# A four-layer network on one core: second layer's routing logits in four groups between the attention lanes' first projections

## The chip, the cores and the metric

The kernel runs on one core of a Trainium2 chip. The time is the device time of one execution, in microseconds. Five engines have a queue of instructions each, carried out in order: TensorE (PE, whose weight loads are shown apart as PEld), VectorE (DVE), ScalarE (ACT), GpSimd (POOL), and SyncE (SP), which issues DMAs. An instruction can wait for a semaphore that another engine raises; whatever stands behind it in its queue waits with it.

## The reference, cut to what matters

Four layers follow one another on 2048 rows of 128 numbers. Each layer normalises the rows (`xn = (x - mean) / sqrt(var + eps)`), computes an attention branch `s` and a feed-forward branch `g` from them, and ends with `x = x + s * g`. The second layer is the one touched:

```
# attention branch, 8 batches of 256 rows
xn2 = layernorm(xn) * ln_scale + ln_bias
hid = silu(xn2 @ W_hidden + b_hidden)          # 128 -> 512
v, gate = hid[..., :256], hid[..., 256:]
qk  = silu(xn2 @ W_qk + b_qk)                  # 128 -> 128
q, k = qk * os_weight[0] + os_bias[0], qk * os_weight[1] + os_bias[1]
a   = square(relu(q @ k.T / 256))
s   = ((a @ v) * gate) @ W_out + b_out
# feed-forward branch: 8 experts, top 2, at most 320 rows an expert
logits = xn @ Wr + br
w = softmax(top 2 of logits); each expert keeps its 320 greatest weights
g = silu(layernorm(xn + sum of the chosen experts' weighted outputs) * gamma + beta)
```

## The kernel before, in words

A stage is a class with one generator for each engine. `Net.run` weaves the generators of its stages: for each engine it takes one step of each generator in turn, up to the next `yield`, until all are through. So a `yield` fixes the order of the instructions in an engine's queue, and nothing else does: there is no planner. A round below is one turn of this weaving; the rounds of PE, DVE and ACT are counted each by themselves, from the start of one `n.run(...)`.

The second layer (`layer1`, L2159) runs, in this order: `Norms` (both normalisations of the rows: `xn` by DVE, the doubly normalised `t1` by ACT), `Turn` as `n.turn` (PE turns `xn` in four quarters of 512 rows through PSUM banks 4 to 7, and DVE copies them into `xT`), `Turn` as `n.inner` (the same for `t1`, banks 0 to 3, copied by ACT into `tT` with gain and bias, L595), and then one run that weaves three stages, `n.run(route, *lanes)`.

**The lanes** are two `SquaredAttention` stages (L1729). Lane 0 takes batches 0, 2, 4, 6 in banks 0 to 2, lane 1 takes 1, 3, 5, 7 in banks 3 to 5 and begins one round later (`later`). On PE a lane has four steps for a batch: the first projections (`qk` L1769, `v` L1771, `gate` L1774), the scores (L1779), their product with `v` (L1786), the output projection (L1793). On DVE it has, after an empty first step, the bias of `v` (L1836), the square (L1839), the gating (L1845), the output rows (L1848); each needs the PE step of its own kind, and the PE step that follows it needs it: the square is needed by the product with `v`, the gating by the output projection, the rows by the next batch's first projections. The scores need `k`, which ACT makes (L1808).

**The routing** is `Route1` (L1926). PE: the 16 logits products of 128 rows each into bank 6 (`pe_logits`, L645), two yields, 16 transposes of the spread weights in two steps (L1961), then eight steps with one count each (L1967), the threshold's product (L1971), and the ranks (L1975, L705, L706). DVE: the logits with bias (L651), the top two, the pair softmax, the spread, copies of the turned weights, and eight rounds of a search for each expert's threshold: in each, DVE reads back the count before (L2040, L2043), sets a candidate (L2032), compares 2048 numbers with it (L2035), and writes `hit` (L2037), which the count on PE needs; after the search the ranks and slots, and the map of rows (`RowMap`), whose last cast (L1922) releases the gathers of the experts' rows on POOL (L1196). DVE takes the routing's step, then lane 0's, then lane 1's in each round, and `hit` of count s (from 0 to 7) is written in its round 5 + s. On PE the order of stages in a round is the same.

In the listing, PE's queue is built by `SquaredAttention.pe_steps` and `Route1.pe`.

Of the kernel before, what the change touches and what calls it, by code (L numbers as in the profile page):

```python
# [13 lines left out]
NB, NS = 8, 256  # L14
NT = NB * NS // P
TOK = NB * NS
E = 8
# [38 lines left out]
def later(lane, idle):  # L56

    for _ in range(idle):
        yield
    yield from lane  # L60
# [176 lines left out]
class Stage:  # L237
# [9 lines left out]
    def pe(self):  # L247
        yield
# [381 lines left out]
class Router(Stage):  # L630
# [9 lines left out]
    def pe_logits(self, tileT, weight, sources, bank):  # L640
        pe, k = self.tensor, weight.shape[1]
        for s in sources:
            pe.wait_ge(*s)
        for t in range(NT):
            ins = pe.matmul(self.n.bank(bank)[:, t * k:(t + 1) * k], tileT(t), weight, start=True, stop=True)  # L645
        ins.then_inc(*self.lg_mm.up())
# [54 lines left out]
    def pe_prefix(self, k, marks, bank):  # L701
        pe, ps = self.tensor, self.n.bank(bank)
        flat = marks[:, :, :].rearrange("p t e -> p (t e)")
        pe.wait_ge(*self.asked.at(k))
        pe.matmul(ps[:, 0:128], self.c["before"], flat, start=True, stop=True)  # L705
        pe.matmul(ps[:, 128:256], self.c["ones"], flat, start=True, stop=True).then_inc(*self.summed.up())  # L706
# [210 lines left out]
class GeluExperts(Stage):  # L917
# [53 lines left out]

    def pe(self):
        pe, N, bank, tb, yb = self.tensor, self.TILES, self.n.bank, self.turn_banks, self.y_banks
        for s in self.sources:
            pe.wait_ge(*s)
# [753 lines left out]
class SquaredAttention(Stage):  # L1729
# [30 lines left out]
    def pe_steps(self):  # L1760
        n, pe, w1 = self.n, self.tensor, self.n.w1
        b0, b1, b2 = self.banks
        for q in range(4):
            pe.wait_ge(*n.inner.done(q))
        for i, b in enumerate(self.batches):
            tT = n.tT[:, b * NS:(b + 1) * NS]
            if i:
                pe.wait_ge(*self.rows.at(i - 1))
            pe.matmul(b2[:, 0:NS], w1["qk"], tT, start=True, stop=True).then_inc(*self.qk_mm.up())  # L1769
            for r in range(2):  # L1770
                ins = pe.matmul(b1[:, r * NS:(r + 1) * NS], tT[:, r * 128:(r + 1) * 128], w1["hidden"][:, 0:256], start=True, stop=True)  # L1771
            ins.then_inc(*self.v_mm.up())
            for f in range(2):
                ins = pe.matmul(b0[:, f * NS:(f + 1) * NS], w1["hidden"][:, 256 + 128 * f:384 + 128 * f], tT, start=True, stop=True)  # L1774
            ins.then_inc(*self.gate_mm.up())
            yield
            pe.wait_ge(*self.k.at(i))
            for r in range(2):
                ins = pe.matmul(b2[:, r * NS:(r + 1) * NS], self.kk[:, r * 128:(r + 1) * 128], self.qT, start=True, stop=True)  # L1779
            ins.then_inc(*self.scores.up())  # L1780
            yield
            pe.wait_ge(*self.a.at(i))
            pe.wait_ge(*self.v_silu.at(i))
            for f in range(2):
                for j in range(2):
                    ins = pe.matmul(b0[:, f * NS:(f + 1) * NS], self.vb[:, j * NS + f * 128:j * NS + f * 128 + 128],  # L1786
                                    self.ab[:, j * NS:(j + 1) * NS], start=(j == 0), stop=(j == 1))
            ins.then_inc(*self.av.up())
            yield
            pe.wait_ge(*self.gated.at(i))  # L1790
            for r in range(2):
                for f in range(2):
                    ins = pe.matmul(b2[:, r * 128:(r + 1) * 128], self.ogT[:, f * NS + r * 128:f * NS + r * 128 + 128],  # L1793
                                    w1["out"][:, f * 128:(f + 1) * 128], start=(f == 0), stop=(f == 1))
            ins.then_inc(*self.out_mm.up())
            yield
# [129 lines left out]
class Route1(Router):  # L1926
# [23 lines left out]

    def pe(self):
        n, pe, c = self.n, self.tensor, self.c
        self.pe_logits(n.xT_tile, n.w1["router"], [n.turn.done(q) for q in range(4)] + [n.w_in["w1"].at(0)], 6)
        yield
        yield
        for q in range(4):
            pe.wait_ge(*(self.spread_a if q >= 2 else self.spread_d).at(0))
            if q >= 2:
                pe.wait_ge(*(self.out_a if q % 2 else self.out_d).at(0))
            for r in range(4):  # L1960
                ins = pe.transpose(n.bank(6 + q % 2)[:, r * 128:(r + 1) * 128], n.t1[:, 4 * q + r, :], c["ident"])  # L1961
            ins.then_inc(*self.turned.up())
            if q % 2:
                yield
        for s in range(8):
            pe.wait_ge(*self.reached.at(s + 1))
            pe.matmul(n.bank(7, 1), c["digit_sum"], self.hit, start=True, stop=True).then_inc(*self.counted.up())  # L1967
            yield
        pe.wait_ge(*self.reached.at(9))
        for i in range(2):  # L1970
            ins = pe.matmul(n.bank(7)[:, 8 * i:8 * i + 8], self.both16[:, 128 * i:128 * i + 128], c["digit_first"], start=True, stop=True)  # L1971
        ins.then_inc(*self.counted.up())
        yield
        pe.wait_ge(*self.reached.at(10))
        pe.matmul(n.bank(7, E), c["ones"], n.e8[0][:, :], start=True, stop=True).then_inc(*self.counted.up())  # L1975
        self.pe_prefix(0, n.tie, 6)
        yield
        self.pe_prefix(1, n.k8[4], 6)
        yield from later(self.map.pe(), 3)
# [179 lines left out]
def layer1(n, before):  # L2159
    norms = Norms(n, n.xn, n.t1, lambda t: [before.done(t)])  # L2160
    n.run(norms)
    n.turn = Turn(n, n.xn, lambda q: n.xT[:, 2 * q:2 * q + 2, 1:1 + NS], norms.once_done, banks=(4, 5, 6, 7), by_dve=(0, 1, 2, 3))
    n.run(n.turn)
    n.inner = Turn(n, n.t1, lambda q: n.tT[:, q * 512:(q + 1) * 512], norms.twice_done, n.w1["ln_g"], n.w1["ln_b"])
    n.run(n.inner)
    kept = KeepRows(n, [norms.once_done(NT - 1)])
    n.run(kept)
    route = Route1(n)
    lanes = [SquaredAttention(n, lane, range(lane, NB, 2), lane) for lane in range(2)]
    n.run(route, *lanes)  # L2170
    experts = FullExperts(n, n.ys[1], [lane.done() for lane in lanes], [n.cleared[1].at(0), kept.kept.at(0), route.map.made.at(0)], route.map)
    n.run(experts)
    got = Back(n, [n.t1, n.g], n.ys[1], experts.done(), "full")
    n.run(got)
    norm = WeightedNorm(n, n.t1, n.g, lambda t: [got.done(t)])
    n.run(norm)
    n.run(Ready(n, ACT.Silu))
    gate = TurnedGate(n, norm.done, n.w1["gamma"], n.w1["beta"])
    n.run(gate)
    return gate  # L2180
# [1575 lines left out]
def build(nc, ins, out):  # L3756
    n = Net(nc, ins, out.rearrange("(t p) c -> p t c", p=P))
    before = layer0(n)
    before = layer1(n, before)
    n.run(Load3(n))  # L3760
    before = layer2(n, before)
    layer3(n, before)
# [103 lines left out]
```

## Time and profile before

| | us |
|---|---|
| three runs | 917.67, 923.87, 923.76 |
| median | 923.76 |
| span of the profiled execution | 921.0 |
| PE busy | 692.4 (75%) |
| DVE busy | 595.3 (65%) |
| ACT busy | 399.3 (43%) |
| POOL busy | 292.5 (32%) |
| second layer's weaving of routing and lanes | 235.6 to 315 |

The three runs bear no mark that tells which of them the profile belongs to; the span is counted from the first to the last instruction, and the median lies 2.8 us above it. The shares are averages over four layers that are each limited by something else, so they say little about one stage. In the traces, a matmul on 32-bit numbers stands as two records, so that the 16 logits products are shown as "x32".

### The profile page before, as it was taken

How to read it: one execution, taken by the hardware profiler on the slowest of the kernel's cores; microseconds unless marked ns; L12 is line 12 of the kernel's file. 1: busy time of each engine (PE TensorE's matmuls, PEld its weight loads, DVE VectorE, ACT ScalarE, POOL GpSimd, SP SyncE). 2: the span in 40 equal slices, each digit the busy share in tenths (PEclk: the TensorE clock that was granted, in tenths of full speed). 3: DMA queues.
4: the chain of work that ended last, by engine and by line, in shares of the span. 5: the costliest groups of instructions: out<-in, count | busy, mean ns of one | idle time of the engine just before them, and what ended most of it. 6: DMA issues, size and time to landing. Idle time of an engine off the chain costs nothing. (4 is left out here: it accounts for less than half of the span.)

```text
span 921.0 us, 14463 instructions
## 1 busy us (share of the span) xinstructions
PE 692.4 (75%) x4255; PEld 516.3 (56%) x4255; DVE 595.3 (65%) x1590; ACT 399.3 (43%) x990; POOL 292.5 (32%) x303
## 2 busy tenths in 40 slices
PE   4999866743979379328986988999976677749991
PEld 2999834632767248327875674656544444426560
DVE  4797487538688611286667567889947665636685
ACT  3201334534735123164444446767756333326660
POOL 1373143540000265300100002445410555665552
PEclk9999878865799779768997899999997699969996
DMA  9991001220100140319008431222100122112515
GB/s 286 244 281 77 1 27 44 68 69 0 47 0 1 11 47 9 93 51 391 1 1 156 124 86 34 75 78 73 53 25 17 48 61 60 57 54 57 163 58 141
DMA packets 79564, 72.97 MB, mean 79 GB/s; under 512 B 9618, under 2 KB 73885, under 8 KB 78977
## 3 DMA queue, kind: packets, MB, share of 16 engines
q1 hardware_dynamic: 68000, 57.56, 23.3%
q0 software_dynamic: 7072, 12.40, 5.2%
q10 hardware_dynamic: 4416, 2.10, 0.9%
q8 instruction: 37, 0.61, 0.3%
q14 instruction: 39, 0.31, 0.1%
HBM read 42.85 MB, written 27.46 MB: 76 GB/s over the span
## 5 line engine op out<-in xcount | busy, mean ns | idle before, releaser
L3493 POOL DMA_INDIRECT ys<-work,back_to x78 | 78.9, 1011 | 83.7 <-DVE work L3452 38.0
L3336 PE MATMUL banks<-weights,work 128*128 x156 | 91.6, 673 | 7.8 <-issue 6.2
L2535 DVE TENSOR_REDUCE work<-banks 128x2 f32<-128x512 f32 x128 | 83.5, 683 | 14.4 <-PE banks L2526 13.1
L3349 PEld LDWEIGHTS banks<-consts,work 128*128 128x128 f32 x156 | 21.8, 155 | 79.4 <-issue 52.5
L3359 PE MATMUL banks<-weights,work 128*128 x312 | 54.8, 303 | 5.4 <-DVE work L3452 3.2
L3349 PE MATMUL banks<-consts,work 128*128 128x128 f32 x156 | 34.3, 305 | 32.1 <-DVE work L3441 15.5
L816 POOL DMA_INDIRECT xs<-t,idx x48 | 49.1, 1023 | 28.7 <-DMA ys<-work,back_to 15.4
L2526 PE MATMUL banks<-work 96*128 96x256 bf16 x256 | 49.3, 277 | 9.1 <-DVE work L2535 6.0
L1196 POOL DMA_INDIRECT g<-rows,back_to x16 | 15.3, 958 | 120.4 <-DVE back_to L1922 115.8
L3359 PEld LDWEIGHTS banks<-weights,work 128*128 128x128 f32 x312 | 46.2, 213 | 8.1 <-issue 7.7
L2939 PE MATMUL banks<-work 99*128 99x256 bf16 x256 | 48.7, 275 | 1.7 <-issue 1.6
L3391 ACT ACTIVATE work<-work 128x256 f32<-128x256 f32 x39 | 16.2, 415 | 69.2 <-DVE work L3429 51.4
L3427 DVE TENSOR_TENSOR work<-banks,weights 128x512 f32<-128x512 f32 x39 | 27.0, 692 | 24.1 <-PE banks L3336 10.9
L816 POOL DMA_INDIRECT xs<-weights,idx x32 | 31.4, 982 | 28.2 <-PE banks L2939 25.7
L3033 ACT ACTIVATE tT<-banks 128x512 f32<-128x512 f32 x64 | 36.5, 598 | 7.5 <-PE banks L2939 5.2
L885 PE MATMUL banks<-consts,g 128*128 128x128 f32 x32 | 7.4, 427 | 41.3 <-DVE g L417 41.3
L2526 PEld LDWEIGHTS banks<-work 96*128 96x128 bf16 x256 | 20.8, 98 | 28.3 <-DVE work L2535 12.6
L3336 PEld LDWEIGHTS banks<-weights,work 128*128 128x128 f32 x156 | 25.8, 207 | 15.6 <-issue 14.8
L567 PE MATMUL banks<-consts,xn 128*128 128x128 f32 x48 | 11.7, 438 | 29.7 <-DVE xn L417 20.1
L3377 ACT ACTIVATE work<-banks,weights 128x128 f32<-128x128 f32 x74 | 30.6, 414 | 7.7 <-PE banks L3317 5.2
L3033 ACT ACTIVATE weights<-banks 128x512 f32<-128x512 f32 x48 | 28.5, 593 | 11.8 <-PE banks L2939 10.5
L1161 ACT ACTIVATE work<-banks,weights 128x320 f32<-128x320 f32 x32 | 16.3, 527 | 39.7 <-PE banks L1135 19.2
(508 smaller groups left out, 1946.1 us busy)
## 6 DMA issues: line engine op xcount, KB each, us to landing
weights<-in_w SPq DMA_DIRECT2D x1, 6668.0 KB, 19.6
weights<-in_w SPq DMA_DIRECT2D x1, 4569.5 KB, 33.8
work<-xs SPq DMA_DIRECT2D x62, 64.5 KB
weights<-in_r SPq DMA_DIRECT2D x1, 2950.5 KB, 26.5
xs<-zero SPq DMA_DIRECT2D x1, 2600.0 KB, 26.1
xs<-zero SPq DMA_DIRECT2D x1, 2580.0 KB, 33.5
work<-xs SPq DMA_DIRECT2D x39, 65.0 KB
weights<-in_w SPq DMA_DIRECT2D x1, 2124.5 KB, 12.1
```

Source lines behind the costliest of these rows:

```text
L816: g.indirect_dma_start(self.table[:, :], bass.IndirectOffsetOnAxis(ap=idx[:, j, t:t + 1], axis=0), self.rows[:, t, :], None, **more).then_ ...
L1161: a.activation(self.hid[e % 2][:, f, :], n.bank(2 + f, cap), ACT.Gelu, bias=n.w1["b1"][:, 4 * e + f:4 * e + f + 1]).then_inc(*self.a.up())
L2526: ins = pe.matmul(ps[:, r * NS:(r + 1) * NS], q[0:self.ROWS, h * NS + r * 128:h * NS + r * 128 + 128], k[0:self.ROWS, h * NS:(h + 1) * NS] ...
L2535: v.tensor_reduce(self.mxb[:, 2 * h:2 * h + 2], self.n.bank(bank).rearrange("p (r n) -> p r n", r=2), AX, ALU.max, negate=True).then_inc(* ...
L2939: ins = pe.matmul(ps[:, kt * NS:(kt + 1) * NS], k[0:h.ROWS + 3, hd * NS + kt * 128:hd * NS + kt * 128 + 128], q[0:h.ROWS + 3, hd * NS:(hd ...
L3033: a.activation(h.PT[s % 8], bank(2 + s % 3), ACT.Exp, scale=float(np.float32(8.0) ** np.float32(-0.5))).then_inc(*h.exp.up())
L3336: pe.matmul(self.mid(t), self.hT[t % 4], w1[:, bass.ds(off * 4, 512)], start=True, stop=True).then_inc(*self.prod1.up())
L3349: ins = pe.transpose(self.mid(m)[:, 128 * f:128 * f + 128], self.ha[m % 4][:, 128 * f:128 * f + 128], self.c["ident"])
L3359: ins = pe.matmul(self.y_bank(m), self.at_[m % 4][:, 128 * f:128 * f + 128], w2[:, bass.ds(self.pe_off[m] * 2 + 128 * f, 128)], start=(f = ...
L3377: a.activation(self.hT[t % 4], self.turn_bank(t), ACT.Identity, scale=gain, bias=bias).then_inc(*self.xT.up())
L3427: v.tensor_tensor(hm, self.mid(t), n.r3["mlp1_b"][:, bass.ds(off * 4, 512)], ALU.add).then_inc(*self.sum.up())
L3493: g.indirect_dma_start(ys[:, :], bass.IndirectOffsetOnAxis(ap=n.back_to[:, t:t + 1], axis=0), self.yb[t % self.RETURNS], None, bounds_chec ...
```

## The change

`Route1.pe` no longer calls `pe_logits`. It waits for the weights, and then for each quarter q in turn for `n.turn.done(q)` alone, issues the four logits products of that quarter, and yields. The last product raises the same semaphore as before. Of the two yields that followed, one stays. `SquaredAttention.pe_steps` no longer waits for all four quarters of `tT` ahead of everything: each batch waits for the quarter that it lies in, `n.inner.done(b // 2)`. For the first batch of a lane, waits are added for what had used its three banks before (the list `free`), and two yields are added: one between the `v` and the `gate` products, and one between the two `gate` products. In `layer1`, the quarters are turned through the banks in another order. The steps of DVE, ACT, POOL and SP are as before, and so is each product.

```diff
--- before.py
+++ after.py
@@ -1760,18 +1760,24 @@
     def pe_steps(self):
         n, pe, w1 = self.n, self.tensor, self.n.w1
         b0, b1, b2 = self.banks
-        for q in range(4):
-            pe.wait_ge(*n.inner.done(q))
+        free = [n.inner.done(q) for q in range(3)] if self.lane == 0 else [n.turn.done(2), n.turn.done(1), n.inner.done(3)]
         for i, b in enumerate(self.batches):
             tT = n.tT[:, b * NS:(b + 1) * NS]
-            if i:
-                pe.wait_ge(*self.rows.at(i - 1))
+            pe.wait_ge(*n.inner.done(b // 2))
+            pe.wait_ge(*(self.rows.at(i - 1) if i else free[0]))
             pe.matmul(b2[:, 0:NS], w1["qk"], tT, start=True, stop=True).then_inc(*self.qk_mm.up())
+            if i == 0:
+                pe.wait_ge(*free[1])
             for r in range(2):
                 ins = pe.matmul(b1[:, r * NS:(r + 1) * NS], tT[:, r * 128:(r + 1) * 128], w1["hidden"][:, 0:256], start=True, stop=True)
             ins.then_inc(*self.v_mm.up())
+            if i == 0:
+                yield
+                pe.wait_ge(*free[2])
             for f in range(2):
                 ins = pe.matmul(b0[:, f * NS:(f + 1) * NS], w1["hidden"][:, 256 + 128 * f:384 + 128 * f], tT, start=True, stop=True)
+                if i == 0 and f == 0:
+                    yield
             ins.then_inc(*self.gate_mm.up())
             yield
             pe.wait_ge(*self.k.at(i))
@@ -1950,8 +1956,14 @@
 
     def pe(self):
         n, pe, c = self.n, self.tensor, self.c
-        self.pe_logits(n.xT_tile, n.w1["router"], [n.turn.done(q) for q in range(4)] + [n.w_in["w1"].at(0)], 6)
-        yield
+        pe.wait_ge(*n.w_in["w1"].at(0))
+        for q in range(4):
+            pe.wait_ge(*n.turn.done(q))
+            for t in range(4 * q, 4 * q + 4):
+                ins = pe.matmul(n.bank(6)[:, t * E:(t + 1) * E], n.xT_tile(t), n.w1["router"], start=True, stop=True)
+            if q == 3:
+                ins.then_inc(*self.lg_mm.up())
+            yield
         yield
         for q in range(4):
             pe.wait_ge(*(self.spread_a if q >= 2 else self.spread_d).at(0))
@@ -2159,9 +2171,9 @@
 def layer1(n, before):
     norms = Norms(n, n.xn, n.t1, lambda t: [before.done(t)])
     n.run(norms)
-    n.turn = Turn(n, n.xn, lambda q: n.xT[:, 2 * q:2 * q + 2, 1:1 + NS], norms.once_done, banks=(4, 5, 6, 7), by_dve=(0, 1, 2, 3))
+    n.turn = Turn(n, n.xn, lambda q: n.xT[:, 2 * q:2 * q + 2, 1:1 + NS], norms.once_done, banks=(6, 4, 5, 7), by_dve=(0, 1, 2, 3))
     n.run(n.turn)
-    n.inner = Turn(n, n.t1, lambda q: n.tT[:, q * 512:(q + 1) * 512], norms.twice_done, n.w1["ln_g"], n.w1["ln_b"])
+    n.inner = Turn(n, n.t1, lambda q: n.tT[:, q * 512:(q + 1) * 512], norms.twice_done, n.w1["ln_g"], n.w1["ln_b"], banks=(2, 1, 0, 3))
     n.run(n.inner)
     kept = KeepRows(n, [norms.once_done(NT - 1)])
     n.run(kept)
```

## Rows read from the trace of the kernel before

**Rows 1.** Head of the profile's page: the span.
```profile
span 921.0 us, 14463 instructions
```

**Rows 2.** Waits, 228 to 320 us: waiter, waited for, us in total, times, longest.
```profile
POOL g L1196 <- DVE back_to L1922: 115.8, 1, 115.8
...
DVE byexpert L651 <- PE banks L645: 5.2, 1, 5.2
```

**Rows 3.** Timeline 228 to 246 us: start, duration, engine, line, operation, idle before.
```profile
234.57 2.76 ACT L595 ACTIVATE tT<-banks,weights 128x512 f32<-128x512 f32 x4
235.61 4.42 PE L645 MATMUL banks<-weights,xT 128*128 128x8 f32 x32
...
239.88 1.20 PE L1769 MATMUL banks<-tT,weights 128*128 128x256 f32 x2
240.14 0.29 DVE L651 TENSOR_TENSOR byexpert<-banks,weights 128x128 f32<-128x128 f32 x1 [5.15 <-PE banks L645]
...
240.88 1.91 PE L1771 MATMUL banks<-weights,tT 128*128 128x256 f32 x4
...
245.55 0.59 PE L1769 MATMUL banks<-tT,weights 128*128 128x256 f32 x2
```

**Rows 4.** Timeline, 258.9 to 288 us: first and last of eight counts, one round between.
```profile
258.90 0.15 DVE L2037 TENSOR_SCALAR work<-work 128x1 f32<-128x1 f32 x1
...
275.16 0.15 DVE L2037 TENSOR_SCALAR work<-work 128x1 f32<-128x1 f32 x1
275.23 0.41 DVE L1848 TENSOR_TENSOR s<-banks,weights 128x256 f32<-128x256 f32 x1
...
275.37 0.38 PE L1967 MATMUL banks<-work,consts 128*128 128x1 f32 x2 [0.74 <-DVE work L2037]
275.56 0.68 DVE L1845 TENSOR_TENSOR work<-banks,work 128x512 f32<-128x512 f32 x1
...
275.70 0.70 PE L1769 MATMUL banks<-tT,weights 128*128 128x256 f32 x2
...
276.16 0.15 DVE L2040 TENSOR_SCALAR work<-banks 128x1 int32<-128x1 f32 x1
...
276.73 2.35 DVE L2035 TENSOR_SCALAR_CACHE_REDUCE work<-work 128x2048 bf16<-128x2048 f32 x1
...
277.96 1.05 PE L1793 MATMUL banks<-weights,work 128*128 128x128 f32 x8
...
279.12 0.15 DVE L2037 TENSOR_SCALAR work<-work 128x1 f32<-128x1 f32 x1
...
287.33 0.15 DVE L2037 TENSOR_SCALAR work<-work 128x1 f32<-128x1 f32 x1
```

**Rows 5.** Timeline, 267 to 271 us: the other two steps of a lane on PE.
```profile
267.46 1.99 PE L1786 MATMUL banks<-work 128*128 128x256 f32 x8 [0.22 <-DVE work L1839]
...
269.29 1.03 PE L1779 MATMUL banks<-work 128*128 128x256 f32 x4
```

**Rows 6.** Timeline, 314 to 316 us: the map's last cast, the first gather.
```profile
314.63 0.18 DVE L1922 TENSOR_SCALAR back_to<-back_to 128x20 int32<-128x20 int32 x1
...
315.64 0.99 POOL L1196 DMA_INDIRECT g<-rows,back_to  x1 [115.83 <-DVE back_to L1922]
```

**Rows 7.** Windows: stretch, length, busy us of each engine, granted clock, DMA.
```profile
236.00:237.00 1.00, 1.00 (x12) 1.00 (x11) 0.00 (x0) 1.00 (x3) 0.00 (x0) 1.00 1.02 291
...
144.00:148.00 4.00, 1.45 (x9) 0.97 (x8) 1.01 (x2) 1.81 (x3) 1.93 (x2) 1.00 0.15 50
258.90:289.40 30.50, 25.67 (x130) 21.03 (x131) 29.46 (x63) 13.62 (x28) 0.00 (x0) 1.00 0.00 1
761.33:764.43 3.10, 0.00 (x1) 0.01 (x1) 1.99 (x6) 0.49 (x2) 1.93 (x4) 0.92 0.05 17
764.43:767.30 2.87, 2.87 (x9) 2.12 (x10) 1.92 (x6) 1.58 (x7) 2.26 (x3) 0.50 0.21 60
...
784.29:787.60 3.31, 3.31 (x9) 2.15 (x10) 1.92 (x6) 1.64 (x7) 2.70 (x3) 0.51 0.23 69
```

## The prediction

> **What bounds the kernel now.** I read four views. First the page's head, for the span of 921.0 us [rows 1]. Then the waits of the stretch that the change touches: POOL stands still for 115.8 us until DVE's cast L1922 [rows 2], and the first gather starts 1 us after it [rows 6]. Nothing else of the second layer follows before that gather, so whatever moves L1922 moves everything behind it. The last rows of a lane (L1848) stand directly behind L1922 in DVE's queue and aren't the later bound by more than their own 0.4 us. Then the timeline from the logits on: PE turns out the 16 logits products between 235.61 and 240.03, DVE waits 5.15 us for them, and only then does PE take lane 0's first projection, at 239.88 [rows 3]. This is the wait that stands out, and quarters of `tT` had been arriving since 235.2 (ACT's four copies begin at 234.57 and take 2.76 us [rows 3]).
>
> Last the timeline of the eight counts [rows 4]: `hit` is written at 258.90 and for the eighth time at 287.33, so a round takes 28.43 / 7 = 4.06 us. In the round shown, DVE writes `hit` (275.16), does lane 0's rows and lane 1's gating, and reads the count back at 276.16, without having waited: PE did the count at 275.37, in 0.38 us, **while** DVE worked for the lanes, and took the lanes' own steps (L1769 at 275.70 and so on) while DVE compared (2.35 us). DVE is busy 29.46 of 30.5 us there, PE 25.67, and the clock is granted in full, 1.00, which is 2.4 GHz [rows 7]. So this stretch is bound by DVE, and only because PE's part of each round lies under the compare.
>
> **The order that the change writes.** PE's queue comes from counting yields. Before, lane 0's step k is in round k, lane 1's in round k+1 (the steps being projections, scores, product, output, projections, ...), and count s in round 5+s. After, a lane's first step takes three rounds, so all later steps come 2 rounds later. The routing's logits take four rounds and one bare yield follows, where there were two rounds: its transposes, counts and the rest come 3 rounds later. DVE's order is not touched. So on PE, the routing slips **one round behind the lanes**:
>
> - before, ahead of count s stand lane 0's step 4+s and lane 1's step 3+s. What these need of DVE stands ahead of compare s.
> - after, ahead of count s stand lane 0's step 5+s and lane 1's step 4+s. These need DVE's step 4+s for lane 0 and 3+s for lane 1, which stand **behind** `hit` s in DVE's queue.
>
> There is no deadlock in it, but a chain: `hit` s, DVE's lane step, PE's step of lane 0, PE's step of lane 1, count s, read back, next compare. What ran beside the compare now runs between two compares, and DVE waits for it with everything queued behind its read-back: the next candidate, compare, and both lanes' steps, hence ACT and PE too.
>
> **A round, priced.** From the end of PE's count to the next `hit` is 0.05 us, then from L2040 to L2035 0.57 us (276.16 to 276.73), the compare with its readout 2.39 us (276.73 to 279.12) [rows 4], in all 3.0. A PE step at full clock takes, from its start to the start of the next: projections 2.26 us (275.70 to 277.96) [rows 4], product 1.83 us (267.46 to 269.29), scores 0.83 and output 0.85 us (their 1.03 and 1.05 less the 0.2 by which successive records overlap) [rows 4, 5]. DVE's lane steps are 0.41 or 0.68 us [rows 4]. Four kinds of round take turns:
>
> - rows, then projections and output: 0.5 + 2.26 + 0.85 + 0.38 + 3.0 = 7.0
> - `v` bias and rows, then lane 1's projections (scores lie under the compare): 1.15 + 2.26 + 0.38 + 3.0 = 6.8
> - square, then product and scores: 0.8 + 1.83 + 0.83 + 0.38 + 3.0 = 6.85
> - gating, then output and product: 0.8 + 0.85 + 1.83 + 0.38 + 3.0 = 6.85
>
> The mean is 6.9 us against 4.06: +2.85 for each of 7 rounds, **+20.0**. Four more waits of the same form follow while lanes still have steps: for the eighth count, the threshold's product, the free places with the first prefix, and the second prefix. Each has a pair of lane steps ahead of it, less what DVE did beside it: 2.65 each, **+10.6**. The row map comes after the lanes' last products and doesn't change.
>
> **The start.** Ahead of the last logits group, PE's queue now holds lane 0's whole first step, and `qk`, `v` and half of `gate` of lane 1. DVE's first routing step needs all four groups, and lane 0's DVE steps stand behind it. At full clock a projection step has 0.59 + two pairs at about 1.03; [rows 3] show 0.59 at 245.55. A logits group is 8 records, at the 12 records a microsecond of 236 to 237 us [rows 7] 0.7 us. Sum: 4 x 0.7 + 2 x 0.59 + 2.06 + 1.03 + 0.5 = 7.6, so the logits end at 243.2 instead of 240.03: +3.2. At half clock, which the before trace has there from 240 on (L1769 as 1.20 and L1771 as 1.91 us [rows 3]), the same list takes 11.3 us: +6.9. I take **+3.2**, since wide products now come between the narrow ones from the start, while the clock stands at 1.00 [rows 7]; +6.9 is kept for the range. The transposes of the spread weights get lane 0's product and lane 1's scores ahead of them: **+0.5**, most of it under the copies.
>
> **What costs nothing.** The waits on quarters and banks: each is for a copy that ended by 237.33 (234.57 + 2.76 [rows 3]), when PE is 1.7 us into its list. If the third quarter weren't there, lane 0's gate would stand for at most 0.7 us. The new bank order changes no count of transposes; the earlier readers of banks 0 to 2 have been done since before the logits. No DMA and nothing of POOL or SP is moved, so nothing is late on their queues but by L1922. The gain of the change, the first `qk` 3.6 us earlier (236.3 instead of 239.88), lands on ACT, whose next lane work waits for DVE anyway: 0.
>
> Sum without the clock: 20.0 + 10.6 + 3.2 + 0.5 = **+34.3**.
>
> **The clock.** In each round PE now sits idle from the count (or the scores behind it) to DVE's next lane step: 3.0 us plus 0.4 to 0.8 of DVE, 3.4 to 3.8, or some 2.8 where scores follow; twelve such gaps. The trace of before has three gaps of 3.1 to 3.4 us in the last layer, and PE resumed at 0.50 (1.2 GHz) after each: after the one at 761.33 it worked 2.87 us at 0.50 [rows 7], at 784.29 it did so again [rows 7], and a third time at 804. That is 2.87 / 2 = 1.4 us lost. Against it: with only 1.45 us of work in 144 to 148 us, the clock stayed at 1.00 [rows 7]. Bounds: none of twelve, 0; all of twelve, 12 x 1.4 = +16.8. I take half of the gaps, **+8.4**, the gaps being like those that cost, but followed by longer bursts.
>
> The Trainium skill has a rule on this, on the page "TensorE: Matmul & The Clock Gate", in the section on HAM oscillation: a TensorE that waits between bursts falls back to half rate in each wait and starts every burst cold. By it the sum would be the upper bound, and the rows at 764 and 784 us agree with it, those at 144 us don't.
>
> **Forecast**: 921.0 + 34.3 + 8.4 = 963.7 us of span; the median of the runs shown is 2.8 us above the span, so 966.5, **966 us**.
>
> **The rivals.**
>
> - *The clock holds* through the gaps: 921.0 + 34.3 + 2.8 = 958. For it the row at 144; against it the three resumptions at 764, 784 and 804.
> - *The clock falls in every gap*: 963.7 + 8.4 + 2.8 = 975, with the half-clock start 979.
> - *The slipped round is hidden.* DVE would find the counts done as before, and only the later logits remained: 923.8 + 3.2 to 6.9 = 927 to 931. For it: PE has 4.8 us of slack in 30.5. Against it: slack is of use only where PE may run ahead, and the steps ahead of each count need what DVE writes after `hit`.
> - *The lanes gain and carry the end*, the other side. Place: the first projections, price: 239.88 - 236.3 = 3.6 us, 920. It decides if the lanes' last rows, not L1922, release the experts by more than 4 us, and no count stands behind a lane step. Against it: L1922 and the last rows lie together, and POOL waits for L1922.
> - *The change doesn't do what it says*: lane 1 finds its bank or quarter busy. All are free by 237.3; worth under 1 us.
>
> **How the numbers follow.** Forecast 0.42, clock holds 0.27, clock falls always 0.20, slip hidden 0.06, lanes carry the end 0.05. The three first all lie far above 1%, which is about what a measurement of this kernel tells from no change, 933 us being the bound: slower 0.89. Both last lie within 1%, less a little for a real gain: same 0.09, faster 0.02. The range leaves the two last out and takes the others with their bounds: from the clock that holds, less the 6 us that the three runs of before spread over, 952, to 979.
>
> **What would show it.** Right: L1967 starts some 3.5 us after L2037 instead of 0.2; DVE shows waits of 2.5 to 3 us at L2040 for PE L1967, eight times, and its busy share of the counts falls from 97% to under 60%; `hit` comes every 6.8 us or more; L651 starts near 243.5; L1922 ends near 349 to 366. The granted clock of the counts' stretch is between 0.75 and 1.00. Wrong: `hit` every 4.1 us, or L651 at 240, or L1967 still directly behind L2037. Then the order of PE's queue isn't the one I counted.

## The result and the profile after

The change makes the kernel slower. Six runs took 970.15 to 976.42 us, 974.43 us in the median, against 923.62 us for the kernel before beside them; the ratio is 1.0582, with a 95% interval of 1.0547 to 1.0617. All ratios here come from fast runs alone, so they can differ a little from the quotient of the two medians (here 1.055). The span of the profiled execution is 973.8 us. The forecast was 966 us, with a range from 952 to 979.

The head of the page of the kernel after:

```profile
span 973.8 us, 14466 instructions
## 1 busy us (share of the span) xinstructions
PE 713.2 (73%) x4255; PEld 531.4 (55%) x4255; DVE 594.7 (61%) x1590; ACT 400.6 (41%) x990; POOL 293.7 (30%) x303
```

DVE, ACT and POOL do the same work in the same busy time. Only PE is busy for longer, 713.2 instead of 692.4 us, with as many instructions. The added time is waiting, and PE's own work stretched.

The waits of the second layer, 228 to 380 us (waiter, waited for, us in total, times, longest), answer to [rows 2]:

```profile
POOL g L1196 <- DVE back_to L1928: 170.0, 1, 170.0
DVE work L2052 <- PE banks L1979: 35.5, 8, 5.1
...
DVE byexpert L651 <- PE banks L1963: 7.9, 1, 7.9
```

L1928 is the cast that was L1922, L2052 the read-back of a count that was L2040, L1979 the count, L1963 the logits. The second row is new: DVE waits for **all eight counts**, 4.4 us each. Before, it waited for none.

The start, in order of time, answers to [rows 3]:

```profile
232.09 0.96 PE L1963 MATMUL banks<-weights,xT 128*128 128x8 f32 x8
...
232.90 0.68 PE L1768 MATMUL banks<-tT,weights 128*128 128x256 f32 x2
...
238.65 0.95 PE L1963 MATMUL banks<-weights,xT 128*128 128x8 f32 x8
...
239.72 0.29 DVE L651 TENSOR_TENSOR byexpert<-banks,weights 128x128 f32<-128x128 f32 x1 [7.87 <-PE banks L1963]
```

The first projection of lane 0 now follows the first logits by 0.8 us, and the last logits end at 239.60, 7.5 us after the first began. Before, it was 4.4 us.

One round of the search (rounds here from one `hit` to the next) answers to [rows 4]:

```profile
277.60 0.15 DVE L2049 TENSOR_SCALAR work<-work 128x1 f32<-128x1 f32 x1
277.67 0.68 DVE L1845 TENSOR_TENSOR work<-work 128x512 f32<-128x512 f32 x1
278.27 0.69 DVE L1842 TENSOR_TENSOR work<-banks,weights 128x512 f32<-128x512 f32 x1
...
278.41 3.78 PE L1792 MATMUL banks<-work 128*128 128x256 f32 x8 [3.81 <-DVE work L1845]
...
281.98 1.09 PE L1785 MATMUL banks<-work 128*128 128x256 f32 x4
...
282.92 0.28 PE L1979 MATMUL banks<-work,consts 128*128 128x1 f32 x2
...
283.23 0.16 DVE L2052 TENSOR_SCALAR work<-banks 128x1 int32<-128x1 f32 x1 [4.27 <-PE banks L1979]
...
283.81 2.35 DVE L2047 TENSOR_SCALAR_CACHE_REDUCE work<-work 128x2048 bf16<-128x2048 f32 x1
...
286.20 0.15 DVE L2049 TENSOR_SCALAR work<-work 128x1 f32<-128x1 f32 x1
```

`hit` is written at 277.60, but the count that needs it starts at 282.92: PE first takes lane 0's product, which waits for the square that DVE does behind `hit`, and lane 1's scores. Before, the count came 0.2 us after `hit`. While DVE compares (2.35 us), PE has nothing to do. The product takes 3.78 us instead of 1.99 [rows 5]: the granted clock of that burst is 0.51 (below).

The granted clock (column ahead of the last two) over the eight counts, then in one gap of PE and in the burst behind it, then in another such pair:

```profile
261.05:320.76 59.71, 34.56 (x118) 28.34 (x118) 28.13 (x55) 14.30 (x28) 0.00 (x0) 0.73 0.00 0
257.90:261.68 3.78, 0.01 (x2) 0.03 (x1) 3.28 (x6) 0.60 (x1) 0.00 (x0) 0.99 0.00 0
261.68:264.50 2.82, 2.82 (x7) 2.28 (x8) 0.45 (x1) 1.50 (x3) 0.00 (x0) 0.50 0.00 0
...
283.20:287.06 3.86, 0.00 (x1) 0.01 (x1) 3.69 (x8) 1.09 (x2) 0.00 (x0) 0.80 0.00 0
287.06:290.50 3.44, 3.44 (x12) 3.17 (x13) 0.54 (x1) 0.00 (x0) 0.00 (x0) 0.50 0.00 0
```

Before, it was 1.00 for the whole of the counts [rows 7], and the same seven rounds took 28.43 us; now they take 59.71, and DVE's busy share there is 28.13 / 59.71 = 47%, from 97%. The end of the stage answers to [rows 6]:

```profile
365.81 0.18 DVE L1928 TENSOR_SCALAR back_to<-back_to 128x20 int32<-128x20 int32 x1
...
366.81 1.00 POOL L1196 DMA_INDIRECT g<-rows,back_to  x1 [169.97 <-DVE back_to L1928]
```

The bill from these rows, in us:

| | before | after | more |
|---|---|---|---|
| start of the trace to the first logits | 235.61 | 232.09 | -3.5 |
| first logits to first `hit` | 23.29 | 28.96 | +5.7 |
| first to eighth `hit` | 28.43 | 59.71 | +31.3 |
| eighth `hit` to the map's last cast | 27.30 | 45.05 | +17.8 |
| from that cast to the end of the span | 606.4 | 608.0 | +1.6 |
| sum | 921.0 | 973.8 | +52.8 |

The bill compares one profiled execution of each kernel. The first row isn't the change's doing: 3.1 of the 3.5 us lie ahead of the second layer's normalised rows, in code that both share, and the rest lies in the turns, which take from 6.8 to 7.3 us from the first normalised row to the first logits in the traces of kernels that turn first, with either bank order.

### The profile page after: what moved, and what is told of

Its sections match the earlier page's. It is cut to its first block and busy times, and to the rows that moved or that the text cites. A ratio compares the mean times of both kernels' runs of the same rounds, so it can differ in the third digit from the quotient of the medians.

```text
span 973.8 us, 14466 instructions
## 1 busy us (share of the span) xinstructions
PE 713.2 (73%) x4255; PEld 531.4 (55%) x4255; DVE 594.7 (61%) x1590; ACT 400.6 (41%) x990; POOL 293.7 (30%) x303
## 5 line engine op out<-in xcount | busy, mean ns | idle before, releaser
L1792 PE MATMUL banks<-work 128*128 128x256 f32 x64 | 27.2, 601 | 17.4 <-DVE work L1845 17.4
L3415 ACT ACTIVATE work<-banks 128x256 f32<-128x256 f32 x78 | 29.2, 375 | 11.1 <-PE banks L3361 7.8
```

## The experiments

All kernels of a group ran on one chip beside the kernel before. In the first group (four kernels) the kernel before took 881.26 us, in the two later ones 921.37 and 921.13 us; the chips differ by some 4.5%, so ratios are compared, and stretches of the traces, which agree between the chips to some 0.1 us for a round.

**The slip undone.** The change without the one bare yield:

```diff
@@ Route1.pe of the change
             if q == 3:
                 ins.then_inc(*self.lg_mm.up())
             yield
-        yield
         for q in range(4):
```

> The change as it is, with the one bare yield behind the routing's logits on PE taken out, so that counts stand as they did before, relative to the lanes' steps. The groups of logits, the waits on quarters and the lanes' two new yields stay. Theory (the slipped round makes the chain): hit every 4.1 us again instead of 8.5, the granted clock at 1.00 through the counts, and only the later logits remain: 924 to 928 us. Rival (the cost lies in the interleaving itself: groups, new waits, the lanes' longer first step): still above 960 us.

It took 887.6 us, 1.0055 (1.0009 to 1.0100) of before. DVE's `hit`, first and last, and the counts' stretch:

```profile
250.16 0.15 DVE L2048 TENSOR_SCALAR work<-work 128x1 f32<-128x1 f32 x1
...
278.59 0.15 DVE L2048 TENSOR_SCALAR work<-work 128x1 f32<-128x1 f32 x1
```

```profile
250.16:278.59 28.43, 24.11 (x118) 19.53 (x118) 27.49 (x55) 12.99 (x27) 0.00 (x0) 1.00 0.00 1
```

The seven rounds take 28.43 us, to the hundredth what they took before, and the clock is back at 1.00. The groups, the new waits, the bank order and the lanes' two yields stay in this kernel, so none of them makes the 50 us. From the first logits to the first `hit` it takes 26.37 us, 3.1 more than before: this is the whole price of the later logits.

**The slip alone.** The kernel before with one yield more:

```diff
@@ Route1.pe of the kernel before
         self.pe_logits(n.xT_tile, n.w1["router"], ... , 6)
         yield
         yield
+        yield
         for q in range(4):
```

> The kernel before with nothing but one bare yield more behind its logits on PE. Theory: the counts slip one round behind the lanes, hit every 8 us or more, DVE waits for each count, and the clock falls in the gaps: 923.6 + 31 for the chain + 12 to 20 for the clock = 966 to 975 us. Rival (the interleaving costs, not the slip): 924 us.

It took 938.6 us, 1.0674 (1.0611 to 1.0737): 57 us slower, by a line that issues nothing. The waits of DVE from the first to the eighth `hit`, and the stretch:

```profile
DVE work L2041 <- PE banks L1968: 31.7, 7, 5.1
```

```profile
252.65:313.46 60.81, 36.02 (x118) 29.50 (x118) 28.13 (x55) 14.30 (x28) 0.00 (x0) 0.71 0.00 0
```

The loss is in full there with the logits in one block, with `hit` every 60.81 / 7 = 8.69 us. It came out above the 966 to 975 us that were expected of the other chip (42 to 51 us more than before). In its trace the way from the first logits to the map's last cast is 54.9 us longer than before: 4.7 up to the first `hit`, 32.4 in the seven rounds, 17.8 behind them. Less the 31 us given to the chain, 24 are left, where I had given the clock 12 to 20. The next run shows that the clock costs more than that in the change; how the 24 us divide in this kernel was not separated.

**The gaps filled.** The change with idle work on PE, behind each count and the threshold's product:

```diff
@@ Route1 of the change
+    def fill(self, k):
+        n, pe = self.n, self.tensor
+        for _ in range(k):
+            pe.matmul(n.bank(6)[:, 0:256], n.w1["qk"], n.tT[:, 0:256], start=True, stop=True)
...
             pe.matmul(n.bank(7, 1), c["digit_sum"], self.hit, start=True, stop=True).then_inc(*self.counted.up())
+            self.fill(5)
             yield
...
         ins.then_inc(*self.counted.up())
+        self.fill(5)
         yield
```

> The change as it is, with five products of 128x256 without use, into a free bank, behind each of the eight counts and behind the threshold's product (some 2 us of work on PE at full clock, in gaps of 3.1 to 3.9 us). Theory (chain plus clock): the clock stays at 1.00 through the counts, hit every 7.0 us instead of 8.5, so 8 or 9 gaps save 1.5 us each: 974.4 - 13 = 961 us, between 958 and 965. Rival A (half clock in the bursts costs nothing, the chain alone is 8.5 us long): 974 us or more. Rival B (the fill delays the next lane step): above 976 us.

It took 920.31 us, 1.0475 (1.0408 to 1.0542), where the change has, on other chips, 1.0582 and, measured again, 1.0618. The 958 to 965 us expected for the first chip are 1.037 to 1.045 of before, so the ratio lies just above them and the quotient of the medians, 1.044, within. One round of it (L1960 is the fill, L2056 writes `hit`, L1984 is the count), and the counts' stretch:

```profile
263.73 0.15 DVE L2056 TENSOR_SCALAR work<-work 128x1 f32<-128x1 f32 x1
...
264.54 1.99 PE L1792 MATMUL banks<-work 128*128 128x256 f32 x8 [1.55 <-DVE work L1845]
266.37 1.03 PE L1785 MATMUL banks<-work 128*128 128x256 f32 x4
267.23 0.28 PE L1984 MATMUL banks<-work,consts 128*128 128x1 f32 x2
267.37 2.40 PE L1960 MATMUL banks<-tT,weights 128*128 128x256 f32 x10
...
267.55 0.16 DVE L2059 TENSOR_SCALAR work<-banks 128x1 int32<-128x1 f32 x1 [2.46 <-PE banks L1984]
```

```profile
248.42:297.99 49.57, 40.06 (x188) 33.40 (x188) 28.14 (x55) 14.19 (x28) 0.00 (x0) 0.97 0.00 0
```

The product is back at 1.99 us, DVE still waits 2.46 us for the count: this is the chain without the clock's part. The rounds took 8.54 us (the first, its gap lying ahead of the first fill), then 6.77, 6.79, 6.87, 7.04, 6.77 and 6.79 us, against 6.8, 6.85, 6.85 and 7.0 worked out for the four kinds, in the order in which they come here. With the clock falling they take 8.53. So more useless work on PE made the kernel some 10 us faster in this stretch (59.71 - 49.57), and half clock costs 1.7 us a round. From the first logits to the map's last cast it takes 120.57 us, in the change 133.72: 13.1 us less, where 13 were expected. That refutes rival A. Rival B is refuted too: in each of the rounds PE waited again for DVE behind the fill (1.55 us in the one shown). Only the step behind the eighth count stood directly behind its fill, and came 2.4 us after that count instead of 1.7.

**DVE slips too.** The change with one yield more on DVE's side, so that both queues have the routing one round behind:

```diff
@@ Route1.dve of the change
         v.tensor_copy(self.spread(0), ...).then_inc(*self.spread_d.up())
         yield
+        yield
         for q in (0, 2):
```

> The change as it is, with one bare yield more in the routing's steps on DVE, behind the spread, so that DVE's search slips one round behind the lanes as PE's counts do. Theory (what costs is the difference between the orders of the two queues): the chain is broken again, hit every 4.1 to 4.3 us, 924 to 929 us. Rival (the counts stand too late in PE's queue as such, whatever DVE's order is): above 960 us.

It took 885.57 us, 1.0061 (1.0023 to 1.0098), 4.3 us more than before by the medians. From the first logits to the first `hit` it takes 28.0 us, 4.7 more than before, and 0.7 less from there to the map's last cast. A `hit` and the count behind it:

```profile
261.55 0.15 DVE L2050 TENSOR_SCALAR work<-work 128x1 f32<-128x1 f32 x1
261.65 0.69 DVE L1851 TENSOR_TENSOR work<-banks,work 128x512 f32<-128x512 f32 x1
261.75 0.38 PE L1979 MATMUL banks<-work,consts 128*128 128x1 f32 x2 [0.78 <-DVE work L2050]
```

```profile
253.53:282.27 28.74, 23.71 (x116) 18.99 (x116) 27.80 (x55) 11.22 (x23) 0.00 (x0) 1.00 0.00 1
```

PE's queue is here, instruction for instruction, that of the slow kernel. What cost 50 us is not where the counts stand in PE's queue but where they stand relative to the same lanes' steps in DVE's.

**Logits earlier.** No slip; a group of logits stands ahead of each quarter of the inner turn, and the lanes' first steps are whole again:

```diff
@@ layer1 and Route1.pe of the change
-    n.run(n.inner)
+    route = Route1(n)
+    n.run(EarlyLogits(n, route), n.inner)    # its pe(): for q: wait turn.done(q), 4 logits products, yield
...
-        pe.wait_ge(*n.w_in["w1"].at(0))
-        for q in range(4):
-            ...
+        yield
         yield
```

> No slip, and the logits earlier instead of later: a group of logits goes ahead of each quarter of the inner turn, the lanes' first steps are whole again and wait for their own quarters. Theory: the one thing worth having at the start is an earlier end of the logits, since DVE waits 5.2 us for them; PE does the same list, so they end some 1 to 3 us sooner after the first turn, the lanes' first projection hardly moves, hit comes every 4.1 us, and the kernel is 0 to 3 us faster than before: ratio 0.997 to 1.000. Rival (the inner turn, now later, holds up the lanes or the spread, which waits for all four quarters): 1 to 4 us slower than before.

It took 925.12 us against 921.37, 1.0040 (1.0007 to 1.0072). The expectation missed: `hit` comes every 4.06 us, but the logits end no sooner. The time is what the rival gave, 1 to 4 us more; the trace shows the clock as well as the later inner turn. Two windows of the logits and turns in this kernel:

```profile
231.00:236.00 5.00, 5.00 (x26) 5.00 (x26) 1.50 (x3) 1.94 (x5) 0.00 (x0) 0.50 0.73 210
236.00:240.00 4.00, 4.00 (x22) 4.00 (x22) 0.00 (x0) 1.55 (x2) 0.00 (x0) 0.50 0.00 0
```

PE was busy all the time and stayed at 0.50, so that a group took 1.71 us, where it takes 0.95 in the change. From the first normalised row (L485) to L651 it took 14.25 us, before 11.74.

**The change again**, beside it on that chip:

> The change as it is, for its ratio on the same chip as the experiments. Theory: hit every 8.5 us again, falls of the clock in every gap, 1.055 to 1.065 of the time before. Rival (the two chips differ in more than a constant): outside of that.

975.96 us, 1.0618 (1.0567 to 1.0669), `hit` every 8.54 us, DVE waiting 35.5 us in eight waits as in the first trace.

**Fill ahead of the layer.** The kernel before, with sixteen useless products of 128x256 on PE once the first layer's gate is through, and four behind the variance:

```diff
@@ layer1 of the kernel before
     n.run(norms)
+    n.run(Fill(n, norms.variance.at(0)))    # PE: 16 products, wait, 4 products, all into bank 0
```

> The kernel before, with twenty products of 128x256 without use on PE in the 9.6 us in which it is idle ahead of the second layer's turns (sixteen at once, four behind the variance). Theory: before, PE starts that layer at half clock (0.50 until 234.8 us) and is at 0.50 again for the end of the logits; kept busy, it turns and makes the logits at 1.00, so that the logits end some 2 to 3 us sooner after the first turn, with hit every 4.1 us as before: ratio 0.997 (0.994 to 1.000). Rival (the clock falls in the logits whatever stands ahead of them, or DVE and ACT pace the turns anyway): no difference that can be told, ratio 0.998 to 1.003.

922.88 us against 921.13, 1.0002 (0.9969 to 1.0035). The clock was at 1.00 through both turns, as wanted, but then:

```profile
234.00:236.00 2.00, 1.81 (x16) 1.66 (x15) 0.11 (x1) 2.00 (x4) 0.00 (x0) 1.00 1.01 290
236.00:238.00 2.00, 2.00 (x14) 2.00 (x13) 0.00 (x0) 1.75 (x2) 0.00 (x0) 0.63 0.20 57
238.00:240.00 2.00, 2.00 (x9) 1.91 (x9) 0.49 (x2) 0.00 (x0) 0.00 (x0) 0.50 0.00 0
```

it fell within the block of logits, which stand from 234.37 us on without a gap. The logits took 5.0 us instead of 4.4, and L651 came 11.95 us after the first normalised row. The rival holds: no difference can be told. Neither of these two kernels is better than the kernel before, and no better one was found.

## Why the prediction was right, point by point

**The order of the queue** was right, and it is the cause: undone, the loss is gone; alone, it is whole; and given to DVE as well, it is harmless. The sign and the place follow from it.

**A round without the clock** was priced at 6.9 us and took 6.77 to 7.04 with the gaps filled. The +20.0 us for seven rounds stands, as (6.84 - 4.06) x 7 = 19.5.

**The tail's four waits** were priced at +10.6. Measured is +17.8 with the clock's part and +14.7 (42.01 - 27.30) in the filled kernel, whose last two gaps had no fill and were still followed by half clock. Its trace tells the two apart:

```profile
313.66 0.29 DVE L714 COPY byexpert<-banks 128x128 f32<-128x128 f32 x1 [0.38 <-PE banks L706]
...
316.77 3.28 PE L1792 MATMUL banks<-work 128*128 128x256 f32 x8 [3.15 <-DVE work L1845]
...
321.80 0.29 DVE L714 COPY byexpert<-banks 128x128 f32<-128x128 f32 x1 [4.48 <-PE banks L706]
...
331.38 0.69 DVE L1851 TENSOR_TENSOR work<-banks,work 128x512 f32<-128x512 f32 x1 [2.86 <-PE banks L1792]
```

From the eighth `hit` to the first of these copies it takes 15.67 us, before 7.94 (287.33 to 295.27), with the granted clock at 1.00: +7.7 for the first three waits (0.7 of it by the fill itself), priced at 7.95. To the second copy it takes 8.14 instead of 3.58, +4.6 for the fourth wait, priced at 2.65, with a product of 3.28 us instead of 1.99 in it. The map's +2.4 (18.20 instead of 15.78), for which I had nothing, goes with the last line: DVE waits 2.86 us for a product in a burst at 0.53, where without the slip it stood idle for 0.5. So the chain was priced about right, and the 4 us over the forecast go with the half clock.

**The start.** The list of 7.6 us of work at full clock ahead of the last logits took 7.5 us, and the first `hit` without the slip came 3.1 us later, where 3.2 was forecast. With the slip it is 5.7; of this, 1.9 us is lane 0's product at half clock, after a gap of 6.6 us in which PE waits for DVE's first routing steps.

**The waits and the bank order cost nothing**, as forecast: both are in the kernel that is 1.0055 of before. Of its whole excess, 4.9 us by the ratio and 6.3 by the medians, 3.1 us lie in the start; where the rest lies was not traced.

**The clock** is the term that was mis-sized. I took half of twelve gaps at 1.4 us, +8.4, and all twelve, +16.8, as its bound. In the change, each of the eleven gaps of PE from 241 us on that last 3 us or more is followed by half clock or runs into it. All of the added time of the stage, 54.8 us, less the 34.3 us of chain and start, leaves 20.5 us, beyond the bound. The parts agree: 1.9 us in the start, 11.8 in the rounds (10.1 that the fill took away and 1.7 of the one gap ahead of it), some 7.2 in the tail (17.8 - 10.6). That is 1.9 us a gap instead of 1.4: the price came from a burst of 2.87 us, and most bursts here are longer.

The page "TensorE: Matmul & The Clock Gate" of the Trainium skill says in its section on HAM oscillation that each burst after such a wait starts cold. This trace agrees in nine of the eleven gaps, where PE starts again at 0.50; behind two of the shorter ones (3.09 and 3.29 us, ending at 270.81 and 305.37) it starts at 1.00 and falls to half some 1.1 and 0.6 us later. So does the third burst of the kernel before that I had read as resumed at half clock: at 804.30 PE starts at 1.00 and is at 0.50 from 805. The stretch at 144 us [rows 7], on which I had counted against the falls, did not carry over.

**The number** owes something to chance. The forecast of 966 us is 8.4 us under the median, though its clock term was 12.1 too small. The rest was made up by the 1.9 us by which this execution was shorter outside of the stage (-3.5 and +1.6 in the bill), and by the median, which lies 0.6 us above the span where 2.8 were added. By the same luck the rival in which the clock falls in every gap gave 975 us, almost the median of 974.4: its clock term was 3.7 us too small.

**The signs.** `hit` every 8.53 us and DVE's share of 47% are as foretold. The count starts 5.3 us after `hit` instead of 3.5, and DVE waits 4.4 us for it instead of 2.5 to 3, since the bursts run at half clock; in the filled kernel it waits 23.0 us in eight waits, 2.9 us each. The granted clock of the counts' stretch, 0.73, lies just outside of the 0.75 to 1.00 given. And L651 at 240 was named as a sign of being wrong: it started at 239.72, but in an execution whose first logits came 3.5 us earlier. From the first logits it is 7.6 us, where 7.9 were foretold and 4.5 were measured before; L1928, at 365.81 near the upper end given, comes 133.7 us after the first logits, where 366 meant 130.4. Such signs are better given as distances than as times.

**What was ruled out.** That the slip is hidden (927 to 931 us): no, PE's slack was of no use. That the lanes' earlier projections carry the end: the first one came 0.8 us behind the first logits instead of 4.3, and nothing ended sooner for it.

## What to carry to other kernels

Where one engine's queue is built by weaving several streams, a pause in one stream shifts it against all the others, and what counts is the order relative to the same streams in the queues of the other engines. Before a yield or a wait is added, write down for one period what stands ahead of the instruction that the bottleneck engine waits for, and which of these items need something that the bottleneck does after its own request: if any does, work that lay beside it becomes a chain. And where such a chain opens gaps of some 3 us on PE, price the bursts behind them at half clock as well: here 1.7 us a round.

## What the runs showed of the hardware

Five useless products added in each gap shortened the rounds from 8.5 to 6.8 us: keeping PE busy paid although the work stood in the queue of the engine that the others waited for.

The clock can also fall while PE is busy without a gap: in the block of 16 products with 8 columns it went from 1.00 to 0.63 and 0.50, though idle time ahead of it had been filled, and in the kernel whose logits alternate with transposes it stayed at 0.50 for 9 us of unbroken work. In the change, where the same logits alternate with products of 256 columns, a group took 0.95 us, with the clock at 1.00 from 231 to 240 us. What in these three orders makes the difference was not isolated; in the change and in the filled block the clock was already at 1.00 ahead of the logits, in the alternating kernel at 0.50.

One chip ran the kernel before in 881 us, the others in 921 to 924, while rounds of the search without the slip took 4.06 us there too. There is no trace of the kernel before on that chip, but those of the four kernels that ran there place the difference: from the second layer's last cast to the end they take 575.5 to 580.4 us, those of the other chips 604.2 to 609.9, and the second layer's first normalised row comes at 212.5 to 218.3 us instead of 225.3 to 228.4. What makes it was not looked into.
